# Twelve buffers for gathered rows in place of six, and table products moved to the end of their TensorE rounds

## The chip, the cores and the metric

One core of one Trainium2 chip runs the whole program, as one launch. The metric is device time in microseconds (us), the median of the runs. All engine names are those of the profile: PE is TensorE, DVE is VectorE, ACT is ScalarE, POOL is GpSimd and SP is SyncE. POOL and SP matter here as the engines that issue transfers.

## The reference, cut to what matters

The program is a small transformer of two layers: a cross-attention, a mixture of experts, a second (windowed) cross-attention, and a quantized feed-forward. The change lies in the mixture of experts alone. There, 1024 tokens of 256 numbers each choose 6 of 32 experts:

```python
scores = jax.nn.sigmoid(x @ gate_w)
... # keep 2 of the 4 groups of experts masked out, take the best 6 experts of the rest
weights = weights / jnp.sum(weights, axis=-1, keepdims=True)
x_exp = jnp.repeat(x, K, axis=0)
sort_idx = jnp.argsort(sel_flat)
xs = x_exp[sort_idx]                              # rows sorted by expert
g = jax.lax.ragged_dot(xs, w_gate, group_sizes)   # 256 -> 176
u = jax.lax.ragged_dot(xs, w_up, group_sizes)
d = jax.lax.ragged_dot(jax.nn.silu(g) * u, w_down, group_sizes)   # 176 -> 256
out = d[unsort_idx].reshape(T, K, H)
expert_out = jnp.sum(out * weights[..., None], axis=1)
shared = jax.nn.silu(x @ sw_gate) * (x @ sw_up) @ sw_down
return (expert_out + shared).reshape(B, S, H)
```

All of it is computed in float32.

## The kernel before

The stages run one after another, with a barrier between them. The stage of the mixture (`experts`, from line 1139) cuts the work into 96 jobs of 128 rows. Jobs 0 to 15 (`SHARED` = 16) are the shared expert, two halves of its hidden width for each of 8 token tiles, and read activations that lie in SBUF. Jobs 16 to 95 are 80 slots (`NSLOT`): each slot is 128 rows of one expert, with rows that must be gathered from the table of normalized tokens in DRAM (`xrow_s`), and weights of the expert that is named only at run time.

PE, ACT and DVE each go through rounds j = 0 to 97, in an order that is written out by hand. Round j on PE before the change is:

- `gate_up(j)` (line 1291): the product with gate and up weights, 352 columns, two chunks of 128 rows;
- `experts_of_tiles` in round 0 only, then `table(j)` in rounds 0 to 7 (line 1272): six products that add to the token table, which says for each slot and lane which token belongs there. It waits for `hot(j)` of DVE, 18 instructions (lines 1392 to 1395) that build the one-hot operands;
- `turn_rows(j + 2 - 16)` in rounds 14 to 93 (line 1279): two transposes of the gathered rows of the slot that is two jobs ahead. It waits for the gather;
- `down(j - 2)` (lines 1308 and 1309): the product with the down weights. It waits for DVE's copy of the transposed hidden rows (`hT`);
- `turn_hidden(j - 1)` (line 1298): two transposes of the hidden rows.

ACT does the silu (line 1333), the copy of the turned rows (line 1338) and the copy of the result (line 1343). DVE's round j before the change is `hot(j)` (j < 8), `hidden(j)` (line 1413, silu times up), `add_shared(j - 2)` (line 1423, jobs of the shared expert), `hidden_turned(j - 1)` (line 1418, the copy to `hT`), `token_table` in round 8 (from line 1400), and in every second round from 28 to 90 one of 32 parts of `quantize` (lines 1445 to 1455, ten linked instructions), which prepares weights of a later stage. A round therefore ends its DVE part with the quantizing, and the next round's `hidden` stands behind it.

POOL issues both indirect transfers, in one program order:

```python
for i in range(XRING - 1):
    gather(i)
pool.wait_ge(s["rows_ready"], 1)
for i in range(NSLOT):
    if i + XRING - 1 < NSLOT:
        gather(i + XRING - 1)
    scatter(i)
```

`gather(i)` (line 1230) fills buffer i modulo `XRING` and waits until the slot that used it was transposed. `scatter(i)` (line 1235) waits for the result of slot i (`y_sb`), which `down` gives in PE's round 18 + i. SP fetches the weights of a slot into a ring of 8 (lines 1205 and 1206), each time that the slot 8 before it has its result. The results go through a ring of 4 (`YRING`): `result(i)` on ACT waits until the scatter of slot i - 4 has landed.

Of the kernel before, what the change touches and what calls it, by code (L numbers as in the profile page):

```python
# [18 lines left out]
TT = TOK // P  # L19
# [69 lines left out]
def wait(eng, sem, value):  # L89

    if not isinstance(value, int) or value > 0:
        eng.wait_ge(sem, value)
# [863 lines left out]
DOWN_HALF = 0.5 - 1.0 / 256  # L956
SHARED = 2 * TT
JOBS = SHARED + NSLOT
WRING, XRING, YRING = 8, 6, 4
CONST = {}  # L960
for _name, _width in (("tri", P), ("before", E_ALL), ("upto", E_ALL), ("lane", P), ("slot", NSLOT), ("tokm", TT), ("spare", NSLOT), ("zero", D)):
    CONST[_name] = slice(sum(c.stop - c.start for c in CONST.values()), sum(c.stop - c.start for c in CONST.values()) + _width)
# [176 lines left out]
def experts(nc, t, x, wabs, wvo, wq):  # L1139

    with Scope(nc, "moe") as sc:
# [54 lines left out]
        with nc.Block() as block:  # L1196
# [50 lines left out]
            def _(pe):  # L1247
# [15 lines left out]
                def experts_of_tiles():  # L1263
                    pe.wait_ge(s["begun_ready"], 1)
                    nc.tensor.matmul(expert_ps, ones[0:E_ALL, 0:E_ALL], begun[:, :], start=True, stop=True).then_inc(s["expert_done"], 1)

                def table(n):
                    pe.wait_ge(s["hot"], n + 1)
                    if n == 0:
                        pe.wait_ge(s["expert_ready"], 1)  # L1270
                    for k in range(TOPK):
                        last = nc.tensor.matmul(token_ps, lane_hot[:, n % 2, k, :], tile_hot[:, n % 2, k, :, :], start=(n, k) == (0, 0), stop=(n, k) == (TT - 1, TOPK - 1))
                    last.then_inc(s["table_part"], 1)

                def turn_rows(i):
                    pe.wait_ge(gathered[i % XRING], 16 * (i // XRING + 1))
                    wait(pe, s["xt_sb"], i - 1)
                    for c in range(DC):
                        last = nc.tensor.transpose(xt_ps[i % 2][:, c * P:(c + 1) * P], xg[:, i % XRING, c * P:(c + 1) * P], ident[:, :])
                    last.then_inc(s["xt_done"], 1)  # L1280

                def gate_up(j):
                    i = j - SHARED
                    wait(pe, s["h_done"], j - 1)
                    if i >= 0:
                        pe.wait_ge(s["xt_sb"], i + 1)
                        pe.wait_ge(load[i % WRING], 32 * (i // WRING + 1))
                    for c in range(DC):
                        rows = xT[:, i % 3, c, :] if i >= 0 else h32[:, c, j // 2 * P:(j // 2 + 1) * P]
                        w = wa[:, i % WRING, :] if i >= 0 else shared_a[:, j % 2, :]  # L1290
                        last = nc.tensor.matmul(up_ps[j % 2][:, 0:GU], rows, w[:, c * GU:(c + 1) * GU], start=c == 0, stop=c == DC - 1)  # L1291
                    last.then_inc(s["up_done"], 1)

                def turn_hidden(j):
                    pe.wait_ge(s["h_done"], j + 1)
                    wait(pe, s["ht_sb"], j - 1)
                    for c in range(2):
                        last = nc.tensor.transpose(ht_ps[j % 2][:, c, :], h[:, j % 2, c * P:(c + 1) * P], ident[:, :])  # L1298
                    last.then_inc(s["ht_done"], 1)

                def down(j):
                    i = j - SHARED
                    pe.wait_ge(s["ht_sb"], j + 1)
                    wait(pe, s["added"], min(j - 1, SHARED))
                    wait(pe, s["y_sb"], i - 1)
                    wd = wa[:, i % WRING, DC * GU:WA] if i >= 0 else shared_a[:, j % 2, DC * GU:WA]
                    we = wb[:, i % WRING, :] if i >= 0 else shared_b[:, j % 2, :]
                    nc.tensor.matmul(y_ps[j % 2][:, 0:D], hT[:, j % 3, 0, :], wd, start=True, stop=False)
                    nc.tensor.matmul(y_ps[j % 2][:, 0:D], hT[0:REST, j % 3, 1, :], we, start=False, stop=True).then_inc(s["y_done"], 1)
# [4 lines left out]
                for j in range(JOBS + 2):  # L1314
                    if j < JOBS:
                        gate_up(j)
                    if j == 0:
                        experts_of_tiles()
                    if j < TT:
                        table(j)  # L1320
                    if 0 <= j + 2 - SHARED < NSLOT:
                        turn_rows(j + 2 - SHARED)
                    if 0 <= j - 2:
                        down(j - 2)
                    if 0 <= j - 1 < JOBS:
                        turn_hidden(j - 1)

            @block.scalar
            def _(act):
# [24 lines left out]
            def _(dve):  # L1354
# [34 lines left out]
                def hot(n):  # L1389
                    wait(dve, s["table_part"], n - 1)  # L1390
                    for k in range(TOPK):
                        V.tensor_scalar(lane_hot[:, n % 2, k, :], const[:, CONST["lane"]], lane_no[:, n, k:k + 1], None, ALU.is_equal)
                        tok = CONST["tokm"].start + n
                        V.tensor_scalar(tile_hot[:, n % 2, k, 0, :], const[:, CONST["slot"]], tile_no[:, n, k:k + 1], const[:, tok:tok + 1], ALU.is_equal, ALU.mult)
                        last = V.tensor_scalar(tile_hot[:, n % 2, k, 1, :], const[:, CONST["slot"]], tile_no[:, n, k:k + 1], float(k - TOPK), ALU.is_equal, ALU.mult)
                    last.then_inc(s["hot"], 1)

                def token_table():
                    dve.wait_ge(s["table_part"], TT)
                    V.tensor_scalar(token_row[:, :], token_ps[:, 0:NSLOT], float(EMPTY), None, ALU.add).then_inc(s["table_ready"], 1)  # L1400
                    link(V.tensor_scalar(turn_no[:, :], token_ps[:, NSLOT:2 * NSLOT], float(TOK), float(UNUSED), ALU.mult, ALU.add))
                    link(V.scalar_tensor_tensor(spare[:, :], turn_no[:, :], float(UNUSED), const[:, CONST["spare"]], ALU.is_equal, ALU.mult))
                    link(V.tensor_tensor(turn_no[:, :], turn_no[:, :], spare[:, :], ALU.add))
                    link(V.tensor_scalar(spare[:, :], token_ps[:, 0:NSLOT], 0.0, float(EMPTY), ALU.is_lt, ALU.mult))
                    link(V.tensor_tensor(turn_no[:, :], turn_no[:, :], spare[:, :], ALU.add))
                    V.tensor_tensor(result_row[:, :], turn_no[:, :], token_ps[:, 0:NSLOT], ALU.add).then_inc(s["rows_ready"], 1)

                def hidden(j):
                    dve.wait_ge(s["silu_done"], j + 1)
                    wait(dve, s["ht_done"], j - 1)  # L1410
                    if j < 2:
                        dve.wait_ge(s["pad_set"], 1)
                    V.tensor_tensor(h[:, j % 2, 0:M], up_ps[j % 2][:, M:GU], silu[:, j % 2, :], ALU.mult).then_inc(s["h_done"], 1)

                def hidden_turned(j):
                    dve.wait_ge(s["ht_done"], j + 1)
                    wait(dve, s["y_done"], j - 2)
                    V.tensor_copy(hT[:, j % 3, :, :], ht_ps[j % 2][:, 0:2, :]).then_inc(s["ht_sb"], 1)  # L1418

                def add_shared(j):  # L1420
                    dve.wait_ge(s["y_done"], j + 1)
                    wait(dve, s["added"], j)
                    V.tensor_tensor(x[:, j // 2, :], x[:, j // 2, :], y_ps[j % 2][:, 0:D], ALU.add).then_inc(s["added"], 1)
# [42 lines left out]
                for j in range(JOBS + 2):  # L1466
                    if j < TT:
                        hot(j)
                    if j < JOBS:
                        hidden(j)  # L1470
                    if 0 <= j - 2 < SHARED:
                        add_shared(j - 2)
                    if 0 <= j - 1 < JOBS:
                        hidden_turned(j - 1)
                    if j == TT:
                        token_table()
                    if SHARED + 4 <= j < SHARED + 4 + TOPK:
                        shares(j - SHARED - 4)
                    if j >= SHARED + 12 and j % 2 == 0 and part < PARTS:
                        if part == 0:  # L1480
                            dve.wait_ge(s["w8_in"], 16)
                        quantize(part)
                        part += 1
# [489 lines left out]
```

## Time and profile before

| what | value |
|---|---|
| median of 3 runs | 2142.54 us |
| all runs | 2128.13, 2142.54, 2173.36 us |
| the profiled execution | 2130.99 us |
| its span | 2129.2 us |
| its mean granted PE clock | 0.908 |
| PE busy | 1805.2 us, 85% of the span |
| DVE busy | 1453.1 us, 68% |
| ACT busy | 1074.8 us, 50% |
| POOL busy | 1080.8 us, 51% |

The profiled execution took 1.8 us more than its span, and its own time lies 11.55 us under the median. Times inside the trace are counted from the start of the span. The stage of the mixture runs from about 1429 to 1880 us; its part with rounds from 1431 to 1828 us.

### The profile page before, as it was taken

How to read it: one execution, taken by the hardware profiler on the slowest of the kernel's cores; microseconds unless marked ns; L12 is line 12 of the kernel's file. 1: busy time of each engine (PE TensorE's matmuls, PEld its weight loads, DVE VectorE, ACT ScalarE, POOL GpSimd, SP SyncE). 2: the span in 40 equal slices, each digit the busy share in tenths (PEclk: the TensorE clock that was granted, in tenths of full speed). 3: DMA queues.
4: the chain of work that ended last, by engine and by line, in shares of the span. 5: the costliest groups of instructions: out<-in, count | busy, mean ns of one | idle time of the engine just before them, and what ended most of it. 6: DMA issues, size and time to landing. Idle time of an engine off the chain costs nothing. (4 is left out here: it accounts for less than half of the span.)

```text
span 2129.2 us, 44379 instructions
## 1 busy us (share of the span) xinstructions
PE 1805.2 (85%) x14711; PEld 1352.4 (64%) x14711; DVE 1453.1 (68%) x3940; ACT 1074.8 (50%) x2650; POOL 1080.8 (51%) x1641
## 2 busy tenths in 40 slices
PE   3447999999999999999999999757888887378997
PEld 3425788777777877877877787543544444136884
DVE  7746887877778778778868877646445554456656
ACT  2414766666666666766767766520222222054443
POOL 4413786676667659657756865100345544154110
PEclk8657999999999999999999999956989998676998
DMA  6671022112202202201220203332367766420100
GB/s 264 245 306 71 2 82 82 35 50 82 82 3 82 82 3 82 82 28 57 82 83 2 82 12 101 108 140 81 108 192 215 212 203 180 139 56 9 41 15 24
DMA packets 74760, 202.58 MB, mean 95 GB/s; under 512 B 9945, under 2 KB 40770, under 8 KB 71170
## 3 DMA queue, kind: packets, MB, share of 16 engines
q1 hardware_dynamic: 61346, 163.70, 22.8%
q0 software_dynamic: 9984, 30.42, 4.4%
q10 hardware_dynamic: 3168, 5.24, 0.7%
q8 instruction: 131, 2.15, 0.4%
q14 instruction: 131, 1.07, 0.2%
HBM read 161.67 MB, written 37.66 MB: 94 GB/s over the span
## 5 line engine op out<-in xcount | busy, mean ns | idle before, releaser
L857 DVE TENSOR_TENSOR att_pT<-att_pT 128x512 bf16<-128x512 f32 (+1 forms) x512 | 321.9, 651 | 198.4 <-ACT att_pT L754 195.7
L616 PE MATMUL att_out<-att_V,att_pT 128*128 128x128 bf16 x5760 | 385.9, 219 | 10.0 <-DVE att_pT L857 8.3
L754 ACT ACTIVATE att_pT<-att_pT 128x512 bf16<-128x512 f32 (+1 forms) x512 | 278.3, 572 | 201.4 <-PE att_pT L604 201.4
L616 PEld LDWEIGHTS att_out<-att_V,att_pT 128*128 128x128 bf16 x5760 | 350.2, 98 | 36.7 <-DVE att_pT L857 19.6
L760 ACT ACTIVATE att_prob<-att_scores,att_negmax 128x512 f32<-128x512 f32 (+1 forms) x512 | 329.5, 653 | 15.8 <-DVE att_negmax L846 14.6
L595 PE MATMUL att_scores<-att_K,att_Q 128*128 128x512 bf16 (+1 forms) x1536 | 331.0, 366 | 0.0
L844 DVE TENSOR_REDUCE att_mx<-att_scores 128x1 f32<-128x512 f32 (+1 forms) x512 | 292.2, 631 | 4.6 <-PE att_scores L595 4.5
L604 PE MATMUL att_pT<-att_ident,att_prob 128*128 128x128 f32 x1920 | 278.2, 276 | 17.4 <-issue 17.4
L595 PEld LDWEIGHTS att_scores<-att_K,att_Q 128*128 128x128 bf16 x1536 | 153.0, 100 | 149.0 <-issue 11.0
L555 PE MATMUL att_aux<-att_wkv,att_kvT 128*128 128x256 bf16 x1440 | 188.1, 282 | 42.4 <-DMA att_kvT<-kv_s 21.1
L604 PEld LDWEIGHTS att_pT<-att_ident,att_prob 128*128 128x128 f32 x1920 | 211.5, 142 | 19.1 <-issue 18.2
L555 PEld LDWEIGHTS att_aux<-att_wkv,att_kvT 128*128 128x128 bf16 x1440 | 139.6, 101 | 69.8 <-DMA att_kvT<-kv_s 21.3
L695 POOL TENSOR_TENSOR att_scaled<-att_kvraw,att_kw 128x256 f32<-128x256 f32 x120 | 82.9, 691 | 192.8 <-ACT att_kvraw L735 192.8
L1235 POOL DMA_INDIRECT y_s<-moe_ysb,moe_result_row x80 | 79.2, 990 | 156.8 <-ACT moe_ysb L1343 155.5
L697 POOL TENSOR_TENSOR att_cosd<-att_scaled,att_tab 128x256 f32<-128x256 f32 (+2 forms) x150 | 123.4, 823 | 11.8
L1333 ACT ACTIVATE moe_silu<-moe_up 128x176 f32<-128x176 f32 x96 | 30.4, 317 | 183.8 <-PE moe_up L1291 137.0
L1230 POOL DMA_INDIRECT moe_xg<-xrow_s,moe_token_row x80 | 77.6, 970 | 86.8 <-DVE moe_token_row L1400 62.2
L1291 PE MATMUL moe_up<-moe_wa,moe_xT 128*128 128x352 f32 x320 | 121.1, 506 | 0.0
L709 POOL TENSOR_TENSOR att_rs<-att_rs,att_nhalf 128x2 f32<-128x2 f32 (+2 forms) x150 | 119.4, 796 | 0.0
L735 ACT ACTIVATE att_kvraw<-att_aux 128x512 f32<-128x512 f32 (+1 forms) x128 | 73.1, 571 | 83.9 <-PE att_aux L555 83.3
L1418 DVE COPY moe_hT<-moe_ht 128x256 f32<-128x256 f32 x96 | 40.6, 423 | 100.3 <-PE moe_ht L1298 100.1
L760 ACT ACTIVATION_READ_ACCUMULATOR att_prob<-att_scores,att_negmax 128x1 f32 x512 | 108.8, 212 | 0.0
(299 smaller groups left out, 3286.2 us busy)
## 6 DMA issues: line engine op xcount, KB each, us to landing
moe_wa<-in_wa_l SPq DMA_DIRECT2D x80, 480.0 KB
att_kvT<-kv_s SPq DMA_DIRECT2D x16, 1920.0 KB
att_tab<-tab_s SPq DMA_DIRECT2D x16, 960.0 KB
att_wq<-wq_s SPq DMA_DIRECT2D x16, 512.0 KB
att_wo<-wo_s SPq DMA_DIRECT2D x16, 512.0 KB
kv_s<-prep_kvhl SPq DMA_DIRECT2D x4, 1920.0 KB
prep_kv<-in_ctx_l SPq DMA_DIRECT2D x4, 1664.0 KB, 7.6
moe_y<-y_s SPq DMA_DIRECT2D x8, 768.0 KB, 4.6
```

The lines of the kernel that those rows point to most:

```text
L555: last = nc.tensor.matmul(o, kvT[:, par, a, c, k0:k0 + P], wkv[:, par, w, c, :], start=(c, a, w) == (0, 0, 0), stop=(c, a) == (DC - 1, 1))
L595: last = nc.tensor.matmul(scores[:, lo:lo + n], Q[:, u, a, i, :], K[:, u, w, lo:lo + n], start=(a, w) == (0, 0), stop=a == 1)
L604: last = nc.tensor.transpose(pT_ps[j % 2][:, m, :], prob[:, i % 2, k0:k0 + P], ident[:, :])
L616: last = nc.tensor.matmul(out_ps[:, i % 2, :], pT[:, i % 2, a, k, :], V[:, par, k, w, :], start=(k, a, w) == (0, 0, 0), stop=(k, a) == (KT ...
L695: eng.tensor_tensor(a, raw[:, 0:m, :], weight[:, :].unsqueeze(1).to_broadcast([P, m, HD]), ALU.mult).then_inc(linked, 1)
L697: eng.tensor_tensor(b.rearrange("p m (e f) -> p m e f", e=2), a.rearrange("p m (e f) -> p m e f", e=2), cos.unsqueeze(2).to_broadcast([P, ...
L709: eng.tensor_tensor(scale, scale, nhalf[:, 0:m], ALU.pow).then_inc(linked, 1)
L754: nc.scalar.activation(pT[:, i % 2, 0, 4 * j:4 * j + m, :], pT_ps[j % 2][:, 0:m, :], ACT.Copy).then_inc(s["pt_hi"], 1)
L760: nc.scalar.activation(prob[:, i % 2, lo:lo + n], scores[:, lo:lo + n], ACT.Exp, bias=negmax[:, i % 4:i % 4 + 1], scale=1.0, accum_out=es[ ...
L844: nc.vector.reduce_max(mx[:, i % 2, k:k + 1], scores[:, lo:lo + n], AX.X).then_inc(s["bank_max"], 1)
L857: nc.vector.tensor_tensor(pT[:, i % 2, 1, 4 * j:4 * j + m, :], pT_ps[j % 2][:, 0:m, :], pT[:, i % 2, 0, 4 * j:4 * j + m, :], ALU.subtract) ...
L1291: last = nc.tensor.matmul(up_ps[j % 2][:, 0:GU], rows, w[:, c * GU:(c + 1) * GU], start=c == 0, stop=c == DC - 1)
```

## The change

The ring of buffers for gathered rows grows from 6 to 12, so that POOL issues 11 gathers ahead of its loop where it issued 5, and `gather(i + 11)` where `gather(i + 5)` stood. In rounds 0 to 7, PE does `table(j)` last, after `turn_hidden(j - 1)`, and DVE does `hidden(j)` last, after `add_shared(j - 2)` and `hidden_turned(j - 1)`. From round 8 on both orders are as before.

```diff
-WRING, XRING, YRING = 8, 6, 4
+WRING, XRING, YRING = 8, 12, 4
...
                     if j == 0:
                         experts_of_tiles()
-                    if j < TT:
-                        table(j)
                     if 0 <= j + 2 - SHARED < NSLOT:
                         turn_rows(j + 2 - SHARED)
                     if 0 <= j - 2:
                         down(j - 2)
                     if 0 <= j - 1 < JOBS:
                         turn_hidden(j - 1)
+                    if j < TT:
+                        table(j)
...
                 for j in range(JOBS + 2):
                     if j < TT:
                         hot(j)
-                    if j < JOBS:
+                    elif j < JOBS:
                         hidden(j)
                     if 0 <= j - 2 < SHARED:
                         add_shared(j - 2)
                     if 0 <= j - 1 < JOBS:
                         hidden_turned(j - 1)
+                    if j < TT:
+                        hidden(j)
                     if j == TT:
                         token_table()
```

## Rows read from the trace of the kernel before

**Rows 1.** Window: busy us (instructions) of PE, PEld, DVE, ACT, POOL; clock; DMA; GB/s.

```profile
1434.80:1486.10 51.30, 33.79 (x114) 18.50 (x115) 35.86 (x165) 2.22 (x7) 0.00 (x0) 0.67 0.27 85
```

**Rows 2.** Groups of PE by line, 1503.3 to 1818.4, idle before them last.

```profile
L1279 PE MATMUL moe_xt<-moe_ident,moe_xg 128*128 128x128 f32 x160 | 36.4, 312 | 53.9 <-DMA moe_xg<-xrow_s,moe_token_row 50.3 <-issue 3.6
```

**Rows 3.** Timeline of PE: first of 80 rounds with gathered rows, one unwaited, the last.

```profile
1503.33 1.35 PE L1291 MATMUL moe_up<-moe_shared_a,moe_h 128*128 128x352 f32 x4
...
1511.83 1.35 PE L1291 MATMUL moe_up<-moe_wa,moe_xT 128*128 128x352 f32 x4
...
1514.66 1.35 PE L1291 MATMUL moe_up<-moe_wa,moe_xT 128*128 128x352 f32 x4
...
1818.37 1.35 PE L1291 MATMUL moe_up<-moe_wa,moe_xT 128*128 128x352 f32 x4
```

**Rows 4.** Timeline of all engines, one round that waits for its gathered rows.

```profile
1719.22 0.99 POOL L1235 DMA_INDIRECT y_s<-moe_ysb,moe_result_row  x1 [2.21 <-ACT moe_ysb L1343]
...
1720.52 0.97 POOL L1230 DMA_INDIRECT moe_xg<-xrow_s,moe_token_row  x1 [0.31 <-PE moe_xt L1279]
...
1721.76 0.42 DVE L1418 COPY moe_hT<-moe_ht 128x256 f32<-128x256 f32 x1 [0.96 <-PE moe_ht L1298]
...
1722.10 0.23 DVE L1445 TENSOR_SCALAR moe_magic<-moe_w 128x144 int32<-128x144 int32 x1
...
1723.35 0.97 POOL L1230 DMA_INDIRECT moe_xg<-xrow_s,moe_token_row  x1 [0.30 <-issue]
...
1725.21 0.34 DVE L1413 TENSOR_TENSOR moe_h<-moe_up,moe_silu 128x176 f32<-128x176 f32 x1
1725.66 0.20 PEld L1279 LDWEIGHTS moe_xt<-moe_ident,moe_xg 128*128 128x128 f32 x2 [3.32 <-DMA moe_xg<-xrow_s,moe_token_row]
```

**Rows 5.** Timeline of the last rounds, where `down` waits for DVE's copy.

```profile
1823.79 0.42 DVE L1418 COPY moe_hT<-moe_ht 128x256 f32<-128x256 f32 x1 [0.74 <-PE moe_ht L1298]
...
1824.27 0.70 PE L1308 MATMUL moe_y<-moe_wa,moe_hT 128*128 128x256 f32 x2 [0.52 <-DVE moe_hT L1418]
...
1826.00 0.42 DVE L1418 COPY moe_hT<-moe_ht 128x256 f32<-128x256 f32 x1 [1.79 <-PE moe_ht L1298]
```

**Rows 6.** Windows: the middle of the slots, and one in which only weights load.

```profile
1575.00:1775.00 200.00, 164.31 (x617) 88.88 (x618) 107.72 (x362) 55.25 (x154) 100.28 (x103) 0.95 0.71 208
1445.00:1450.00 5.00, 2.55 (x12) 1.46 (x13) 2.82 (x14) 0.00 (x0) 0.00 (x0) 0.83 1.04 342
```

**Rows 7.** DMA queues and issues, 1575 to 1775: packets, MB, share of 16 engines.

```profile
q1 hardware_dynamic: 10756, 27.89, 50.9%
q0 software_dynamic: 4978, 13.61, 20.0%
...
moe_wa<-in_wa_l SPq DMA_DIRECT2D x51, 480.0 KB
```

**Rows 8.** Timeline of PE in the rounds with table products (8 rounds; first products, a slow and a fast round, the end).

```profile
1447.45 0.59 PE L1272 MATMUL moe_xt<-moe_tile_hot,moe_lane_hot 128*128 128x160 f16 x6 [2.93 <-DVE moe_tile_hot L1395]
...
1462.31 0.98 PE L1272 MATMUL moe_xt<-moe_tile_hot,moe_lane_hot 128*128 128x160 f16 x6 [1.77 <-DVE moe_tile_hot L1395]
...
1470.10 0.59 PE L1272 MATMUL moe_xt<-moe_tile_hot,moe_lane_hot 128*128 128x160 f16 x6 [1.76 <-DVE moe_tile_hot L1395]
...
1476.28 0.98 PE L1272 MATMUL moe_xt<-moe_tile_hot,moe_lane_hot 128*128 128x160 f16 x6 [2.93 <-DVE moe_tile_hot L1395]
...
1484.07 0.59 PE L1272 MATMUL moe_xt<-moe_tile_hot,moe_lane_hot 128*128 128x160 f16 x6 [1.76 <-DVE moe_tile_hot L1395]
...
1486.11 2.56 PE L1291 MATMUL moe_up<-moe_shared_a,moe_h 128*128 128x352 f32 x4
```

**Rows 9.** Timeline of DVE in the same stretch.

```profile
1465.41 0.42 DVE L1423 TENSOR_TENSOR all_x<-all_x,moe_y 128x256 f32<-128x256 f32 x1 [2.91 <-PE moe_y L1309]
1466.03 0.42 DVE L1418 COPY moe_hT<-moe_ht 128x256 f32<-128x256 f32 x1 [0.20 <-PE moe_ht L1298]
1469.95 0.34 DVE L1413 TENSOR_TENSOR moe_h<-moe_up,moe_silu 128x176 f32<-128x176 f32 x1
```

## The prediction

> **What bounds the kernel now.** I read the views in this order: the windows by stage, then the groups of TensorE by line in the stage that the change touches, then the timeline of that stage round by round, and last the DMA queues. The stages follow each other behind barriers, so only what shortens the mixture's own rounds counts. Two stretches matter.
>
> The slots. From round 14 to round 94 there are 80 rounds with gathered rows, and they take 1818.37 - 1503.33 = 315.04 us [rows 3], 3.94 us each. The reader should then look for a round in which TensorE waits for nothing: 1511.83 to 1514.66, 2.83 us [rows 3]. So 315.04 - 80 x 2.83 = 88.6 us are not work at full clock. The group of the transposes of gathered rows names the cause: TensorE was idle for 53.9 us just before them, 50.3 of it ended by the gather's DMA [rows 2]. The rest, 34.7 us, is rounds at a lower granted clock (0.95 in the middle of the stretch, [rows 6]) that come after a long wait. Both go if the waits go.
>
> Why the gather is late shows in one such round [rows 4]. POOL works in program order: the scatter of a slot starts at 1719.22, when that slot's result is there, and behind it, at 1720.52, the gather that is six slots further. TensorE wants it in its second round after, and starts on it at 1725.66, having waited 3.32 us in its weight-load queue. The gather needed 5.1 us from issue. The ring's depth sets this: gather i + 6 stands behind the result of slot i (PE's round 18 + i), and is transposed in round 20 + i.
>
> The table rounds. From round 0 to 7, the clock is 0.67 and DVE is busy for 35.86 of 51.3 us [rows 1]. DVE builds the one-hots, TensorE waits for them (idle before the products 1.76 to 2.93 us), and only behind the products come the down product and the transposes, for which DVE waits in turn: 2.91 us before the addition [rows 8, 9]. The two engines take turns.
>
> **The change, part by part: the ring.** With 12 buffers gather i + 12 stands behind the result of slot i and is transposed in round 26 + i: six rounds more, 17 us or more on top of the two that held 5.1 us with a wait of 3.32. That is past anything in these rows, so the DMA wait goes in full. What is late next has to be found among the others in the round.
>
> TensorE itself: 2.83 us a round [rows 3].
>
> POOL: gather and scatter, 1.30 us from one start to the next [rows 4], 2.6 us a round. That is under 2.83, so it holds, by 0.2 us. The 11 gathers at the start take 11 x 1.3 = 14 us from the token table on. The first transpose doesn't come before six rounds after the table, as before, and needs only the first gather; those behind it come at 1.3 us each against 2.83 us for a round. Cost: nothing.
>
> DVE, in the 64 rounds 28 to 91, where every second round has a part of the quantizing. After the copy to hT (1721.76) the ten instructions of the part run, and hidden starts at 1725.21: 3.45 us [rows 4]. Then hidden itself 0.34 us and the next copy to hT 0.42 us [rows 4]. The down product of that slot waits for this copy. Where it is seen to wait, it starts at 1824.27, 0.06 us after the copy's end (1823.79 + 0.42), and the next copy starts at 1826.00, 1.73 us after the down product [rows 5]. This loop is closed: 3.45 + 0.34 + 0.42 + 0.06 + 1.73 = 6.00 us for two rounds, or 3.00 us a round, against 5.66 for TensorE. It is slightly longer than TensorE's own work and so becomes the bound. It is hidden today because rounds take 3.94 us.
>
> The DMA engines: 51 slots in 200 us keep them busy for (50.9% + 20.0%) x 200 / 51 = 2.78 us a slot [rows 7], with 208 GB/s at a share of 0.71 [rows 6]. This is under 3.00 us, but at 93% of it. A cheaper bound: while nothing but weights was loading, 342 GB/s went at a share of 1.04 [rows 6], 329 GB/s at one; the slot's (27.89 + 13.61) / 51 = 0.81 MB would take 2.5 us. The weights are asked for five rounds ahead, 14 us or more, so a burst is absorbed and only the mean counts. I take the DMA engines as not bounding, and keep 2.78 plus a tenth for contention, 3.06 us, as near end, and 3.5 us as far end.
>
> So the slots take 16 x 2.83 + 64 x 3.00 = 237.3 us, and the ring gives 315.0 - 237.3 = 77.7 us. If DVE's loop were shorter than I read it, 80 x 2.83 = 226.4 us and a gain of 88.6. TensorE then waits at most 0.34 us in two rounds, much less than the waits of 2 to 3 us that stood ahead of the low clock, so I count every round at full clock.
>
> **The order in the table rounds.** Now TensorE does gate_up, down and turn_hidden while DVE builds the one-hots, and the six products last. Of each round, DVE's part is the one-hots (1466.45 to 1469.95, 3.50 us), an addition and a copy of 0.42 us each, and hidden, 0.34 us [rows 9]: 4.68 us. TensorE's part is its step less its wait: 7.79 - 1.76 = 6.03 us at the low clock, and 6.18 - 2.93 = 3.25 us at full clock [rows 8]. The engines now overlap, so a round is the longer of both: 4.68 us at full clock, about 6.0 at the low one. Neither level will hold: in rows 8 TensorE came up to full clock behind a busy stretch, and fell back behind a wait of 2.93 us, and the new round has a wait of 4.68 - 3.25 = 1.4 us at full clock. I take the middle, 5.3 us. Before, five steps took 1484.07 - 1447.45 = 36.62 us, 7.32 each [rows 8]. The gain is 5 x (7.32 - 5.3) = 10.1 us, with 6.6 (all at the low clock) and 13.2 (all at full clock) as ends. Rounds 0 to 2 have no down products between; I give them 0.5 us. At the end, gate_up(8) came 2.04 us after the last table products began [rows 8], behind down and transposes; now it comes right behind them, in 0.4 to 0.8 us: 1.4 us. In all 12 us, from 8 to 15. DVE's hidden now stands behind two waits on TensorE; ACT's silu for it is long ready, and turn_hidden needs it only a round later, so nobody waits for the move. The token table starts DVE's round-8 tail as before and has six rounds of cover.
>
> **The sum.** 2130.99 (the profiled execution) - 77.7 - 12 = 2041.3 us. The four executions that I can see are 2128.1, 2131.0, 2142.5 and 2173.4; their median is 2136.8, 5.8 us above the profiled one. I carry that over: 2047 us. A difference of 2%, 43 us, is about what a measurement of this kernel can tell from no change.
>
> **The rivals.**
>
> The DMA engines become the bound. For it: 2.78 us of 3.00 are busy already [rows 7], gathers, scatters and weights share the 16 engines, and the gather's 5.1 us [rows 4] shows queueing. Against it: 329 GB/s at a share of one against 0.81 MB in 3.00 us, 270 GB/s. The weights asked for in the rounds from 18 on are 72 slots: at 3.06 us each the stretch takes 72 x 3.06 + 8 x 2.83 = 243 us, 6 us more than the forecast, 2053 us; at 3.5 us it takes 274.6, 2084 us.
>
> POOL is held off by DVE. The rows: the gather at 1723.35 was issued in the midst of a quantizing part that began at 1722.10, and took 0.97 us, as the one at 1720.52 outside of it [rows 4]. If it were held off, two rounds would need 4 x 1.3 us of POOL beside 3.1 us of quantizing in which it couldn't work, 8.3 us, or 4.15 us a round; 64 rounds of this are 64 x (4.15 - 3.94) = 13 us longer than now, the other 16 are 16 x (3.94 - 2.83) = 18 us shorter, and the kernel would end at 2137 + 13 - 18 - 12 = 2120 us. The Trainium skill (page "SBUF — State Buffer", section "SBUF: two separate sides", its box on DVE blocking DMA) says that GpSimd can't write the descriptors of its DMAs while DVE runs an instruction that holds their shared port. By that rule this rival should be the case; the trace speaks against it, as issues go through at 0.97 us, and rounds of less than 4.15 us are common already. At most the landing is delayed, and 12 buffers cover that.
>
> Slower than before: the ring of results. Result i waits until the scatter of slot i - 4 has landed, so four rounds of cover, 11.3 us at 2.83 against 15.8 us at 3.94. If scatters landed later than 11.3 us behind their issue, because faster rounds and gathers far ahead fill POOL's DMA queue, ACT would wait, then the down product, and TensorE would fall to low clock again: 6 us rounds for those hit. From a mean round of (315.0 + 12) / 80 = 4.09 us on the kernel is slower; at 4.8 us it is 2137 + 57 = 2194 us. A landing of 5.1 us speaks against it.
>
> The ring does what it should and the new order nothing: TensorE stays at low clock and waits turn up elsewhere. 2137 - 78 = 2059 us.
>
> No DVE loop: 2137 - 89 - 15 = 2033 us.
>
> **How the numbers follow.** Forecast 2047 us with its own spread from 2033 to 2060, which takes in the last two rivals (0.08 the order without effect, 0.12 no DVE loop), 0.68 in all. The DMA engines bound, 2053 to 2084 us, 0.26. POOL held off, about 2120, 0.03. Results late, 0.03, in a third of it over 2% slower. The range reaches from 2027 (no DVE loop, on the profiled execution: 2131 - 104) to 2075 us, most of the way to the far end of the DMA rival. Over 2% faster is under 2099.7 us, which holds the first two cases: 0.94; within 2% 0.05; slower 0.01.
>
> **What would show it.** In the slots: no DMA wait before the transposes of gathered rows (line 1279), rounds of 2.83 us up to 27, from 28 on pairs of 5.9 to 6.0 us with a short wait of the down product (line 1308) for DVE's copy, clock 1.00, DMA share 0.9 or more. In the table rounds: steps of 4.7 to 6 us, DVE near 95% busy, the wait of the addition (line 1423) for TensorE short or gone. Wrong would be: gate_up (line 1291) waits for weights; POOL's indirect transfers longer than 1.0 us; ACT waits for scatters (line 1343).

## The result, and the profile after

The change takes the kernel from 2135.34 us (median of 4 runs, 2119.52 to 2173.36) to 2030.11 us (4 runs, 2028.21 to 2030.39). The ratio is 0.952, with a 95% interval of 0.9481 to 0.9558; it leaves out the run of 2173.36 us, which was in a slow state. The profiled execution took 2028.21 us with a span of 2026.4 us, against 2130.99 and 2129.2 us before: 102.8 us less of span.

The windows of the kernel after, for the table rounds, the slots, and the middle of the slots (columns as in [rows 1]):

```profile
1434.80:1469.30 34.50, 24.59 (x114) 14.92 (x115) 34.40 (x163) 2.22 (x7) 0.00 (x0) 0.90 0.40 126
1485.10:1720.50 235.40, 234.68 (x962) 136.49 (x961) 153.90 (x503) 77.25 (x236) 143.23 (x146) 1.00 0.84 248
1540.00:1700.00 160.00, 159.33 (x646) 91.78 (x645) 112.06 (x378) 53.01 (x161) 105.85 (x108) 1.00 0.92 270
```

The first row answers to [rows 1]: practically the same instructions (165 and 163 of DVE's) in 34.5 us and not 51.3, DVE busy for 34.40 of the 34.50 us, and a clock of 0.90 where it was 0.67. Taken apart, the clock is 0.73 up to 1440, 0.60 up to 1445, and 1.00 from there on. The second row shows TensorE busy for all but 0.7 of 235.4 us, at full clock. Busy isn't the same as at its peak here, since the ends of its instructions are modelled: the time that the split quantizing saves further down lies inside these 234.68 us.

The groups of the slots, 1485.1 to 1720.5 (idle before them last), answer to [rows 2]:

```profile
L1230 POOL DMA_INDIRECT moe_xg<-xrow_s,moe_token_row x71 | 68.9, 970 | 21.8 <-PE moe_xt L1279 20.9 <-issue 0.9
...
L1279 PE MATMUL moe_xt<-moe_ident,moe_xg 128*128 128x128 f32 x160 | 30.5, 273 | 0.0
L1308 PEld LDWEIGHTS moe_y<-moe_wa,moe_hT 128*128 128x128 f32 x152 | 22.8, 190 | 8.1 <-DVE moe_hT L1418 8.1
```

The 53.9 us of idle time before the transposes of gathered rows are 0.0. In their place the weight load of the down product (PEld is TensorE's weight load) waits for DVE's copy, 8.1 us in all: 32 times, once for each part of the quantizing. POOL's gather still takes 970 ns.

One such loop in the timeline of all engines answers to [rows 4] and [rows 5]:

```profile
1590.81 0.34 DVE L1413 TENSOR_TENSOR moe_h<-moe_up,moe_silu 128x176 f32<-128x176 f32 x1
...
1591.07 0.41 DVE L1418 COPY moe_hT<-moe_ht 128x256 f32<-128x256 f32 x1
...
1591.54 0.30 PEld L1308 LDWEIGHTS moe_y<-moe_wa,moe_hT 128*128 128x128 f32 x2 [0.27 <-DVE moe_hT L1418]
...
1592.80 0.44 PE L1298 MATMUL moe_ht<-moe_ident,moe_h 128*128 128x128 f32 x2
...
1593.27 0.42 DVE L1418 COPY moe_hT<-moe_ht 128x256 f32<-128x256 f32 x1 [1.25 <-PE moe_ht L1298]
...
1593.61 0.22 DVE L1445 TENSOR_SCALAR moe_magic<-moe_w 128x144 int32<-128x144 int32 x1
...
1596.77 0.34 DVE L1413 TENSOR_TENSOR moe_h<-moe_up,moe_silu 128x176 f32<-128x176 f32 x1
```

From one hidden behind a quantizing part to the next, 1590.81 to 1596.77, are 5.96 us for two rounds. Between them stand, in turn, the copy, the down product that waited for it, the transposes, the next copy, and the ten instructions.

The DMA queues, 1540 to 1700, answer to [rows 7]:

```profile
q1 hardware_dynamic: 11119, 28.87, 65.9%
q0 software_dynamic: 5167, 14.11, 25.7%
...
y_s<-moe_ysb,moe_result_row POOLq DMA_INDIRECT x54
moe_xg<-xrow_s,moe_token_row POOLq DMA_INDIRECT x54, 4.6
```

That is (65.9% + 25.7%) x 160 / 54 = 2.71 us of the DMA engines for a slot, where it was 2.78. A gather lands 4.6 us after its issue (median).

The table rounds, timeline of DVE and PE, answer to [rows 8] and [rows 9]:

```profile
1455.43 0.59 PE L1272 MATMUL moe_xt<-moe_tile_hot,moe_lane_hot 128*128 128x160 f16 x6 [1.26 <-DVE moe_tile_hot L1395]
...
1459.76 0.43 DVE L1423 TENSOR_TENSOR all_x<-all_x,moe_y 128x256 f32<-128x256 f32 x1
1459.92 0.59 PE L1272 MATMUL moe_xt<-moe_tile_hot,moe_lane_hot 128*128 128x160 f16 x6 [1.25 <-DVE moe_tile_hot L1395]
1460.09 0.44 DVE L1418 COPY moe_hT<-moe_ht 128x256 f32<-128x256 f32 x1
...
1460.42 0.35 DVE L1413 TENSOR_TENSOR moe_h<-moe_up,moe_silu 128x176 f32<-128x176 f32 x1
```

A round is 4.49 us, and DVE has no idle time before the addition or the copy; TensorE waits 1.26 us and stays at full clock. This holds for rounds 3 to 7.

**Where the 102.8 us of span are.** I take the start of gate_up in rounds 0, 14 and 94 of each trace: 1431.45, 1503.33 and 1818.37 us before, 1430.98, 1485.06 and 1720.56 us after.

| stretch | before | after | less |
|---|---|---|---|
| up to round 0 | 1431.5 | 1431.0 | 0.5 |
| rounds 0 to 13 | 71.9 | 54.1 | 17.8 |
| rounds 14 to 93 (slots) | 315.0 | 235.5 | 79.5 |
| from round 94 to the end | 310.8 | 305.8 | 5.0 |

### The profile page after: what moved, and what is told of

Same layout as the page of the kernel before. It is cut to its first block and busy times, and to the rows that moved or that the text cites. A ratio compares the mean times of both kernels' runs of the same rounds, so it can differ in the third digit from the quotient of the medians.

```text
span 2026.4 us, 44379 instructions
## 1 busy us (share of the span) xinstructions
PE 1757.9 (87%) x14711; PEld 1335.0 (66%) x14711; DVE 1451.1 (72%) x3940; ACT 1069.8 (53%) x2650; POOL 1079.3 (53%) x1641
## 5 line engine op out<-in xcount | busy, mean ns | idle before, releaser
L604 PE MATMUL att_pT<-att_ident,att_prob 128*128 128x128 f32 x1920 | 278.0, 276 | 16.3 <-issue 16.3
L1291 PE MATMUL moe_up<-moe_wa,moe_xT 128*128 128x352 f32 x320 | 107.9, 460 | 0.0
L828 DVE SCALAR_TENSOR_TENSOR att_kjunk<-att_kvraw 128x128 bf16<-128x128 f32 x240 | 85.0, 388 | 0.0
```

The costliest lines, as they stand in the source:

```text
L604: last = nc.tensor.transpose(pT_ps[j % 2][:, m, :], prob[:, i % 2, k0:k0 + P], ident[:, :])
L828: last = nc.vector.scalar_tensor_tensor(kjunk[:, n % 4, q, :], k_rows, 1.0 / HD, k_rows, ALU.mult, ALU.mult, accum_out=kss[:, n % 4, q:q + 1])
```

## The experiments

The kernels ran in three series, and times below are medians of the runs of one series. Each series had runs of the kernel before beside it; the edits are against the changed kernel unless said otherwise. "Slots" is the stretch from round 14 to 94 of the profiled execution.

**Twelve buffers alone** (both orders as before).

```diff
-WRING, XRING, YRING = 8, 6, 4
+WRING, XRING, YRING = 8, 12, 4
```

> Twelve buffers alone, both orders as before the change. My theory (the two parts are independent: the ring is worth the slots' stretch, 315.0 to 235.5 us in the two traces, the order the rounds 0 to 13, 18 us): slots in about 236 us, rounds 0 to 13 in 72 us as before, about 2050 us. Rival (the faster slots need the engines' better clock that the new order gives): slots 245 us or more, over 2058 us.

Measured: 2043.81 us (2040.56 to 2049.34), ratio 0.9592 (0.9545 to 0.9639). Slots 235.5 us, rounds 0 to 13 69.5 us. The gate_up of rounds 14 and 94 in its trace:

```profile
1497.91 1.35 PE L1291 MATMUL moe_up<-moe_shared_a,moe_h 128*128 128x352 f32 x4
...
1733.38 1.35 PE L1291 MATMUL moe_up<-moe_wa,moe_xT 128*128 128x352 f32 x4
```

The ring gives its 79.5 us without the new order. The median came out 6 us under the expectation. Against the kernel before, the profile has 5.5 us less behind the slots (305.3 us) and 2.4 us less in rounds 0 to 13, whose orders are the same in both.

**The order alone** (six buffers).

```diff
-WRING, XRING, YRING = 8, 12, 4
+WRING, XRING, YRING = 8, 6, 4
```

> The new order alone, six buffers. My theory: table rounds in steps of 4.5 us at full clock, the slots as before in about 315 us with 50 us of waits for gathers; about 18 us under the kernel before, 2113 to 2117 us. Rival (the order's gain is lost again at the first gathers, since the token table comes no earlier against the weights): no more than 5 us under the kernel before.

Measured: 2115.68 us (10 runs, 2111.83 to 2126.33), ratio 0.9921 (0.9889 to 0.9952). Table rounds 4.50 us, rounds 0 to 13 54.0 us, slots 319.6 us. The transposes of gathered rows in its groups, 1481.7 to 1801.3:

```profile
L1279 PE MATMUL moe_xt<-moe_ident,moe_xg 128*128 128x128 f32 x160 | 35.7, 307 | 58.8 <-DMA moe_xg<-xrow_s,moe_token_row 58.6
```

The waits for gathers are all there, 58.8 us of them. So the two parts roughly add up: against 2134.13 us in this series, the ring gives 90.3 and the order 18.5 us, together 109 us. Both together gave 105 in the first comparison, and 103.7 in this series (with eight buffers, below). On top of the ring the order is therefore worth 13.4 us here (2043.81 - 2030.40), less than the 18.5 us without it. Of the ring's 90.3 us the slots explain 79.5; the rest lies in stretches that it has no known part in, and differs from trace to trace.

**Six buffers, but gathers ahead of scatters on POOL.**

```diff
-WRING, XRING, YRING = 8, 12, 4
+WRING, XRING, YRING = 8, 6, 4
...
-                for i in range(NSLOT):
+                for i in range(NSLOT + 4):
                     if i + XRING - 1 < NSLOT:
                         gather(i + XRING - 1)
-                    scatter(i)
+                    if i >= 4:
+                        scatter(i - 4)
```

> The change with only six buffers, but on POOL each scatter stands four gathers later: gather(i + 5), then scatter(i - 4), so that a gather waits for its buffer alone and not for a result. My theory (the place behind the scatter made gathers late, and the buffers only buy distance from it): no wait for gathers, the time of the change, 2028 to 2034 us. Rival (six buffers are too few for the landing time): waits for gathers of 30 us or more in all, over 2070 us.

Measured: 2031.55 us (2029.74 to 2031.93), ratio 0.9524 (0.9479 to 0.9568), slots 235.7 us, and no wait for a gather. The timeline of POOL in it:

```profile
1551.65 0.99 POOL L1235 DMA_INDIRECT y_s<-moe_ysb,moe_result_row  x1 [0.86 <-ACT moe_ysb L1344]
1552.95 0.97 POOL L1230 DMA_INDIRECT moe_xg<-xrow_s,moe_token_row  x1 [0.31 <-PE moe_xt L1280]
```

The two instructions follow each other as before (lines of ACT and PE are one higher, as the edit adds a line), but the gather in the second row is now for the slot that is ten behind the scattered one, not six, in the same six buffers. What made gathers late was the result that each stood behind in POOL's program order. The buffers only bought distance from it.

**Eight buffers.**

```diff
-WRING, XRING, YRING = 8, 12, 4
+WRING, XRING, YRING = 8, 8, 4
```

> The change with eight buffers. My theory: a gather starts 4.6 us into its round and is wanted four rounds later, some 7.7 us on, against a landing of 3.6 to 6.2 us: no wait, 2028 to 2034 us, so that four of the twelve buffers buy nothing. Rival (bursts on the DMA engines need the full depth): waits for gathers remain, 2040 us or more.

Measured: 2030.40 us (2029.06 to 2032.90), ratio 0.9519 (0.9474 to 0.9563), slots 235.8 us. Four of the twelve buffers buy nothing.

**Seven buffers, in a series with odd waits.** The next four kernels ran in one series, and ACT, in three of them DVE too, shows waits that no other trace has.

```diff
-WRING, XRING, YRING = 8, 12, 4
+WRING, XRING, YRING = 8, 7, 4
```

> The change with seven buffers. My theory: a gather starts 4.6 us into its round and is wanted 4.9 us later, against landings of 3.6, 4.7 (median), 6.2 us: half of the rounds wait, a few tenths to 1.3 us, and slots take 238 to 250 us; 2033 to 2045 us. Rival (the lower clock behind waits makes it collapse as with six): over 2060 us.

Measured: 2044.81 us (2042.26 to 2047.76), ratio 0.9558 (0.9527 to 0.9589), slots 251.2 us. Who waited for whom, 1482 to 1733 (us in total, times, longest):

```profile
ACT moe_silu L1333 <- remote: 20.9, 6, 3.9
PEld moe_xt L1279 <- DMA moe_xg<-xrow_s,moe_token_row: 19.0, 23, 1.7
...
ACT moe_xT L1338 <- remote: 7.6, 5, 2.3
...
PE moe_xt L1279 <- DMA moe_xg<-xrow_s,moe_token_row: 4.8, 8, 1.1
```

"remote" is what the profile writes where it finds no releaser. The waits for gathers are short (1.7 us at most in the weight-load queue, 4.8 us in all on the matmuls). They came 23 times in 80 rounds, where half of the rounds were expected, and there is no collapse as with six. But what they cost by themselves can't be read off beside 28.5 us of the others: inconclusive for the time.

**The quantizing split, first run.**

```diff
-                def quantize(n):
+                def quantize(n, half):
...
+                    if half == 0:
...
+                        then(V.tensor_scalar(over[:, :], y8[:, :], E4M3_MAX, 3e38, ALU.is_gt, ALU.mult), 5)
+                        return
...
-                    if j >= SHARED + 12 and j % 2 == 0 and part < PARTS:
+                    if j >= SHARED + 12 and part < 2 * PARTS:
...
-                        quantize(part)
+                        quantize(part // 2, part % 2)
```

Instructions 1 to 5 of a part run in one round, 6 to 10 in the next.

> The change with each part of the quantizing cut into two halves of five instructions, one in every round from 28 to 91. My theory (DVE's loop of 5.96 us for two rounds is the bound there): every slot round in 2.83 us, slots in about 226.5 us, 9 us less, about 2021 us. Rival (the DMA engines, busy 2.72 us a slot in the trace of the change, bound next): rounds stay near 2.9 to 3.0 us with waits of gate_up for weights or of transposes for gathers, 2026 to 2031 us.

Measured: 2050.97 us (2048.26 to 2053.92), ratio 0.9588 (0.9557 to 0.9619), slots 255.8 us, with 37 us of waits without a releaser. Taken alone this would refute the loop of DVE. But rounds 14 to 27, in which this kernel does the same as the changed one, took 46.4 us too where they took 39.7, so something other than the edit was at work.

**TensorE's move alone, first run.**

```diff
                     if j < TT:
                         hot(j)
-                    elif j < JOBS:
+                    if j < JOBS:
                         hidden(j)
...
-                    if j < TT:
-                        hidden(j)
                     if j == TT:
```

> The change, but DVE keeps its old order (hidden right after the one-hots); only TensorE's table products move. My theory (TensorE's order alone lets the engines overlap; hidden's silu is ready anyway): as the change within 3 us, 2027 to 2033 us. Rival (hidden ahead of the addition and the copy holds these up and needs its place at the end): 5 us or more slower.

Measured: 2050.33 us (2046.26 to 2051.87), ratio 0.9587 (0.9559 to 0.9616), slots 254.3 us. What such a wait looks like, in the timeline of ACT and PE:

```profile
1481.24 0.32 ACT L1333 ACTIVATE moe_silu<-moe_up 128x176 f32<-128x176 f32 x1 [3.40 <-PE moe_up L1291]
1486.92 0.32 ACT L1333 ACTIVATE moe_silu<-moe_up 128x176 f32<-128x176 f32 x1 [5.37 <-remote]
...
1485.96 0.89 PE L1308 MATMUL moe_y<-moe_shared_a,moe_hT 128*128 128x256 f32 x2 [3.03 <-DVE moe_hT L1418]
...
1488.41 2.55 PE L1291 MATMUL moe_up<-moe_shared_a,moe_h 128*128 128x352 f32 x4
```

TensorE's gate_up began at 1481.36 and took 1.35 us, so the silu could have run at 1482.7. It ran 4.2 us later; TensorE waited, and gate_up of round 15 ran at the low clock (2.55 us for 1.35). The code of this round is that of the changed kernel.

**DVE's move alone.**

```diff
                     if j == 0:
                         experts_of_tiles()
+                    if j < TT:
+                        table(j)
...
                         turn_hidden(j - 1)
-                    if j < TT:
-                        table(j)
```

> The change, but TensorE keeps its old order; only DVE's hidden moves to the end of its round. My theory: the engines still take turns, since down and the transposes stand behind the table products that wait for the one-hots: all of the order's gain is gone, 2046 to 2052 us, table rounds of 6 to 7.8 us. Rival (half of the gain comes from DVE's order): 2040 us or less.

Measured: 2068.91 us (2066.72 to 2070.79), ratio 0.9668 (0.9639 to 0.9697), slots 254.4 us. Its time is inflated by the same waits, so I read only its table rounds, which have none, in the timeline of PE:

```profile
1461.88 0.59 PE L1272 MATMUL moe_xt<-moe_tile_hot,moe_lane_hot 128*128 128x160 f16 x6 [2.03 <-DVE moe_tile_hot L1395]
1468.87 0.59 PE L1272 MATMUL moe_xt<-moe_tile_hot,moe_lane_hot 128*128 128x160 f16 x6 [2.11 <-DVE moe_tile_hot L1395]
1476.02 0.98 PE L1272 MATMUL moe_xt<-moe_tile_hot,moe_lane_hot 128*128 128x160 f16 x6 [2.01 <-DVE moe_tile_hot L1395]
1484.05 0.98 PE L1272 MATMUL moe_xt<-moe_tile_hot,moe_lane_hot 128*128 128x160 f16 x6 [2.00 <-DVE moe_tile_hot L1395]
```

Steps of 6.99, 7.15 and 8.03 us, and rounds 0 to 7 take 57.4 us, where the kernel before has 54.7 the ring alone 52.4, and TensorE's move alone 38.3 us in the same series. The steps go beyond the 7.8 us that were expected at most. DVE's move gives nothing, and the order's gain is TensorE's, which the repeat below confirms.

**The control, in a third series, with two repeats.** No edit in the first; the second and third are the split and TensorE's move alone again.

> The changed kernel itself, unchanged, beside the next three on one chip. In the runs of seven buffers, of the split, and of each order alone, ACT and DVE showed waits of 20 to 40 us in the slots with no releaser in the profile (called remote), which no earlier run had. My theory (a property of the chip of those four runs, not of the kernels): whatever this chip does, the control and the two repeats show it alike. Rival (the edits cause it): the control is free of it, about 2030 us, and the repeats have it.

> The split quantizing again. My theory (DVE's loop bounds the rounds 28 to 91): 9 us under the control if the chip is free of those waits, all slot rounds 2.83 us. Rival (the split costs something itself, as its first run at 2051 us says): slower than the control.

> TensorE's move alone, again. My theory: within 3 us of the control. Rival (DVE's order matters): 5 us or more over it.

Measured: control 2030.83 us (2029.27 to 2031.55); split 2020.60 us (2018.88 to 2023.84), ratio 0.9469 (0.9415 to 0.9522); TensorE's move alone 2030.44 us (2029.80 to 2031.33). None of the three shows a wait without a releaser. The same code took 20 and 30 us more in the series before, so the edits are not the cause. The split is 10 us faster than the control, with no overlap of runs; TensorE's move alone equals the whole change. Middle of the slots with the split, window and timeline of PE:

```profile
1540.00:1700.00 160.00, 160.00 (x680) 95.88 (x679) 119.89 (x395) 55.99 (x171) 107.73 (x110) 1.00 0.94 282
```

```profile
1561.11 1.35 PE L1291 MATMUL moe_up<-moe_wa,moe_xT 128*128 128x352 f32 x4
...
1563.94 1.35 PE L1291 MATMUL moe_up<-moe_wa,moe_xT 128*128 128x352 f32 x4
```

All rounds from 28 to 91 take 2.83 or 2.84 us. In the control they alternate between 2.83 and 3.12, as in these rows of it:

```profile
1560.83 1.35 PE L1291 MATMUL moe_up<-moe_wa,moe_xT 128*128 128x352 f32 x4
...
1563.66 1.35 PE L1291 MATMUL moe_up<-moe_wa,moe_xT 128*128 128x352 f32 x4
...
1566.79 1.35 PE L1291 MATMUL moe_up<-moe_wa,moe_xT 128*128 128x352 f32 x4
```

Slots 226.7 us, 8.8 less than the control's 235.5. TensorE is busy for 160.00 of 160.00 us, and the DMA engines, at 0.94 and 282 GB/s, still hold nobody up.

**Six buffers, gathers first, and the split.** Both edits above together.

> Six buffers, gather(i + 5) ahead of scatter(i - 4), and the split quantizing. My theory: as the split with twelve buffers within 2 us, so the fastest with half of the buffers. Rival (at 2.83 us a round the DMA engines are the bound, and six buffers don't cover it): rounds of more than 2.9 us, 4 us or more over the split with twelve.

Measured: 2021.96 us (2018.13 to 2025.21), ratio 0.9477 (0.9422 to 0.9532), slots 226.7 us. It equals the split with twelve buffers within the spread of the runs, and with the six buffers of the kernel before it is faster than the changed kernel.

## Why the prediction was right, and where its terms were off

The forecast was 2047 us (2027 to 2075), the measured median is 2030.1 us. Mechanisms and sign were right; the sum was 17 us too high. Against the profiled execution it gave 2041.3, and 2028.2 was measured. Of the 17 us, the order makes 5.8, the ring 1.8, the rest of the program 5.5 and the step to the median 3.9. By its steps:

- **The ring, 77.7 us: measured 79.5.** The slots were to take 237.3 us and took 235.5. The waits for gathers went in full, and so did the low clock behind them: 1.00 in the whole stretch. The experiment with twelve buffers alone shows the same 235.5 us.
- **What is late next: DVE's loop, 6.00 us for two rounds: measured 5.96.** The profile shows the wait (8.1 us, 32 times), and the split removes the wait and the loop: 8.8 us of slots and 10 us of time. This is shown. Of its legs, hidden to copy took 0.26 us where I had put 0.34, as the copy's row starts before hidden's has ended, and copy to hidden over the ten instructions 3.50 where I had 3.45.
- **"The ring's depth sets this" is only half of it.** The depth sets it given POOL's order. With scatters four later the same six buffers do as well, and eight do as well as twelve.
- **The order, 12 us: measured 17.8 in rounds 0 to 13, and 18 us by the run with the order alone.** This term was mis-sized, beyond its own end of 15 (16.3 us up to round 8, and 1.5 in rounds 8 to 13). Against the trace of the ring alone, whose rounds 0 to 13 took 69.5 us and not 71.9, it is 15.4 us, so the old order itself doesn't take the same time twice. I took the middle between a round at full clock and one at the low clock, 5.3 us. The rounds from 3 on ran at full clock, and took 4.49 us and not 4.68, again because instructions overlap; that is also under the 4.7 to 6 us that I named as the sign of it. Five rounds of 5.3 - 4.49 us are 4 of the missing 5.8 us. A wait of 1.26 us in each round didn't bring the clock down; in the kernel before waits of 1.76 and 2.93 us stood there. Besides, round 8 ran at the low clock before (2.56 us for its gate_up, [rows 8]) and at full clock after, 1.5 us that I had not counted. That hidden's move costs nothing was right, and it gives nothing either.
- **The rest of the program, 0: measured 5.0 us less behind the slots and 0.5 ahead of round 0, but not from the change.** From round 94 to the end it is 305 to 311 us in all traces: 310.8 before, 305.8 after, 310.4 in the control, 305.3 and 311.0 with the ring and the order alone. It doesn't go with the edits.
- **The median, + 5.8 us: measured + 1.9.** I carried the distance between the profiled execution and the median over. The runs after lie within 2.2 us of each other, those before within 54, or within 23 without the one of 2173.36. So the distance before didn't carry over, which is 3.9 us of the miss. That the waits for gathers and the low clock make the runs before vary is likely, since the new kernel has neither in its slots, but it isn't shown.

One reading in the prediction was off and left the sum as it was. It put the 34.7 us of the slots that are neither work at full clock nor wait down to the low clock, by a clock of 0.95 in the middle. The window of all the slots of the kernel before has 0.92:

```profile
1503.30:1818.40 315.10, 261.24 (x963) 143.33 (x962) 155.29 (x503) 83.53 (x236) 146.11 (x149) 0.92 0.64 186
```

Going through the rounds of that trace, 17 of the 80 have TensorE rows at the low clock, and they are 24 us longer than 2.83 us and their own waits. By the mean clock it can't be much more: 0.92 is half speed in 16% of 315 us, 50 us, which would take 25 us at full speed (an estimate). The other 11 us lie in rounds at full clock, for instance 0.23 us in the one from 1721.56 to 1727.37, beside its wait of 2.75 and 2.83 us of work. All of it went with the waits, so the gain was the same.

The rivals: the DMA engines were not the bound, at 2.71 us a slot and even in rounds of 2.83 us. POOL was not held off by DVE: its gathers kept 970 ns while DVE was busy for 75% of the time (119.89 of 160 us with the split). The result ring never made ACT wait for a scatter. The rule of the Trainium skill (page "SBUF — State Buffer", section "SBUF: two separate sides"), that GpSimd can't write its DMA descriptors while DVE holds their shared port, doesn't show in issue times here. It isn't refuted either, as a part of the quantizing is ten instructions of 0.22 to 0.35 us, and no row tells which of them hold the port. The effect might lie in the landing: gathers landed 2.8 us after issue (median of 1482 to 1492, while no weights move) and 4.6 us in the middle of the slots. There the DMA engines are also at 0.92, and no run tells the two apart.

What stays open is the cause of the waits without a releaser in the second series. They came in four kernels of one series, all between rounds 14 and 94. In three of the kernels they stopped ACT and DVE together in round 14, where the share of the DMA engines was 0.3 to 0.4; later most of them were on ACT. Many ended about 9.5 us or twice that behind each other, with seven buffers at 1527.23, 1536.77, 1546.32 and 1565.13, and in the split at 1612.43, 1622.05, 1631.72 and 1641.35 us, though the rounds of the two differ. No row tells what has that period. The kernel before had 2140.9 us there against 2134.1 and 2137.9 in the other series, no difference beyond the spread of its runs. The record gives the same chip number, 5, for the second series and for the third, in which the control and both repeats were free of the waits. A lasting property of that chip, my theory beside the control, thus doesn't fit; a passing state of it may.

## What to carry to other kernels

When a transfer is late, ask what stands ahead of it in its issuing engine's program order before adding buffers: here six buffers with the gathers moved four results ahead did what twelve did in the old order. When the largest wait goes, add up the next closed loop across engines from the trace's own rows, since a helper task in bulk (3.1 us of quantizing in every second round) becomes the bound as soon as rounds are short, and cutting it in two removes it again. When two engines take turns, put what waits for the slower one last in the faster one's round.

## What the runs showed of the hardware

The low clock adds to the waits that stand before it: in the slots of the kernel before, 53.9 us of waits came with 24 us more in 17 rounds at the low clock, and the ring took both. In the table rounds it was dearer than the wait itself: TensorE's part of a round took 6.03 us at the low clock against 3.25 us, with a wait of 1.76 us [rows 8]. Waits of 1.26 us in rounds of 4.49 us left the clock at full in the new table rounds, while waits of 1.8 to 2.9 us in rounds of 6 to 8 us went with a clock of 0.67. The 16 DMA engines went at a mean share of 0.94 and 282 GB/s for 160 us, with weights, gathers and scatters mixed, without holding anyone up. And with TensorE's move alone the slots took 254.3 us in one series and 235.5 in another: the same kernel, 19 us apart.
